# Slot attention stage of a decoder kernel on one Trainium2 core: four groups in turn in place of two, three units at once in a beat

## What is computed

```python
Pn = rmsnorm(P, input_norm_w); k_proj = Pn @ Wk.T; v_proj = Pn @ Wv.T
for _ in range(3):
    q_proj = rmsnorm(slots, slot_norm_w) @ Wq.T
    scores = einsum("bkd,bmd->bkm", q_proj, k_proj) * SCALE
    attn = softmax(scores, axis=-2)
    attn = attn / (sum(attn, axis=-1, keepdims=True) + EPS)
    updates = einsum("bkm,bmd->bkd", attn, v_proj)
    slots = gru_cell(updates, slots, ...)   # r, z: sigmoid; n = tanh(xn + r * hn)
x = layernorm(x + slots)
route = sigmoid(x @ Wr + br)                # the expert with the highest route takes the token
```

## Time and profile before

| | us |
|---|---|
| median of 3 runs | 1671.12 |
| the profiled execution, its own time | 1671.58 |
| its span, first to last instruction | 1669.4 |
| `slot_stage` | 918 to 1479 |
| TensorE busy over the span (89%) | 1489.2 |
| VectorE busy (76%) | 1262.5 |
| ScalarE busy (66%) | 1105.3 |
| POOL busy (75%) | 1246.7 |

### The profile page before, as it was taken

How to read it: one execution, slowest core, us unless ns; L and a number is a source line. 1 busy time by engine, 2 the same in 40 slices (tenths; PEclk the granted TensorE clock), 3 DMA queues, 4 the chain that set the end, 5 groups by cost and what they waited for, 6 DMA issues and landing times. The chain is left out here.

```text
span 1669.4 us, 22143 instructions
## 1 busy us (share of the span) xinstructions
PE 1489.2 (89%) x6336; PEld 908.0 (54%) x6336; DVE 1262.5 (76%) x2184; ACT 1105.3 (66%) x2134; POOL 1246.7 (75%) x884
## 2 busy tenths in 40 slices
PE   4889899989999999989987999999999999929994
PEld 1334334433443343433432777777777777729993
DVE  2999999999999999999996466666666675644552
ACT  4778887788778887888775665556556565414553
POOL 2899999999999999999996435666566655534665
PEclk8999999999999999999999899999999999959997
DMA  5455555554555455555551840412403310036771
GB/s 175 136 192 183 164 175 176 180 173 158 198 165 187 156 180 193 182 163 176 169 174 44 269 167 17 154 44 111 154 25 130 103 48 14 7 87 189 214 208 39
DMA packets 126058, 236.93 MB, mean 142 GB/s; under 512 B 13490, under 2 KB 76917, under 8 KB 125952
## 3 DMA queue, kind: packets, MB, share of 16 engines
q1 hardware_dynamic: 121408, 227.21, 41.8%
q0 software_dynamic: 4544, 8.47, 1.5%
HBM read 180.89 MB, written 55.66 MB: 142 GB/s over the span
## 5 line engine op out<-in xcount | busy, mean ns | idle before, releaser
L388 POOL TENSOR_TENSOR hc<-state,c_rows 128x1024 f32<-128x1024 f32 x256 | 599.1, 2362 | 50.0 <-DVE state L585 40.3
L585 DVE TENSOR_TENSOR_SCAN state<-ps_da,inp 128x512 f32<-128x512 f32 x512 | 593.5, 1207 | 29.6 <-ACT ps_da L481 29.6
L704 PE MATMUL ps_y<-hc,ident 128*128 128x512 f32 x1024 | 495.1, 623 | 55.5 <-POOL hc L388 55.4
L481 ACT ACTIVATE ps_da<-dt,a_neg 128x512 f32<-128x512 f32 x512 | 345.1, 688 | 81.7 <-DVE state L585 79.2
L704 PEld LDWEIGHTS ps_y<-hc,ident 128*128 128x128 f32 x1024 | 195.6, 198 | 298.8 <-issue 214.7
L574 DVE TENSOR_TENSOR inp<-dtx,ps_b 128x1024 f32<-128x1024 f32 x192 | 230.9, 1203 | 39.3 <-POOL dtx L359 23.0
L998 POOL TENSOR_TENSOR rs<-ms,m_half 128x4 f32<-128x4 f32 x48 | 49.7, 1035 | 186.4 <-DVE ms L1201 186.4
L371 POOL TENSOR_TENSOR inp<-dtx,b_rows 128x1024 f32<-128x1024 f32 x64 | 150.9, 2358 | 0.1
L627 PE MATMUL ps_misc<-x1T,w_conv 128*128 128x512 f32 (+3 forms) x256 | 118.6, 608 | 20.9 <-ACT x1T L414 20.9
L487 ACT COPY ps_b<-b_rows 128x512 f32<-128x512 f32 x192 | 111.1, 579 | 36.6 <-DVE inp L574 35.1
L1662 POOL DMA_INDIRECT out_x<-orow,target x78 | 77.0, 987 | 43.4 <-ACT orow L1681 23.7
(11 more groups left out here) (214 smaller groups left out, 2759.9 us busy)
## 6 DMA issues: line engine op xcount, KB each, us to landing
b_rows<-bc_rows SPq DMA_DIRECT2D x128, 512.0 KB, 4.7
c_rows<-bc_rows SPq DMA_DIRECT2D x128, 512.0 KB, 4.0
sorted_x<-pad_rows SPq DMA_DIRECT2D x8, 4160.0 KB, 16.3
w<-in_L_ffn_W SPq DMA_DIRECT2D x78, 256.0 KB
vw<-vw_rows SPq DMA_DIRECT2D x16, 462.0 KB
vw_rows<-vw_out SPq DMA_DIRECT2D x16, 384.0 KB
xrow<-sorted_x SPq DMA_DIRECT2D x39, 130.0 KB, 2.3
x_tok<-in_x SPq DMA_DIRECT2D x16, 256.0 KB, 4.0
```

The costliest lines, as they stand in the source:

```text
L388: pool.tensor_tensor(hc[:, n % RING], state[:, n % RING], over_c(c_rows[:, slot, n % 2]), ALU.mult).then_inc(hc_ready, 1)
L481: act.activation(ps_da[u % DA_RING][:], dt[:, par, c], ACT.Exp, scale=a_neg[:, c, n:n + 1]).then_inc(da_ready, 1)
L585: dve.tensor_tensor_scan(state[:, n % RING, c], ps_da[u % DA_RING][:], inp[:, n % RING, c], 0.0, ALU.mult, ALU.add).then_inc(state_ready, 1)
L704: ins = pe.matmul(ps_y[:, c], ident[:], hc[:, n % RING, c], start=False, stop=n == NS - 1)
```

## The change

The units of four groups follow each other: iteration 0 of groups 0 to 3, iteration 1 of groups 0 to 3, iteration 2, and then the next four. Each beat n holds the attention half of unit n up to the exponentials, the second part of the attention of unit n-1 (`den` to `weights`), and the GRU half of unit n-2, whose last steps (`gate_new`, `kept`, `mixed`, `new_h`) fall in beat n+1 of the loop as unit n-3. An iteration of a group therefore spans four beats. There are 48 beats with units and nine more in the loop. A group is routed in single steps, from `residual` at its ready beat (offset 0) to `scatter` (offset 6). For the first three fours, groups become ready three beats apart; the last four become ready in beats 47 to 50.

PSUM banks belong to a step and not to a lane: `ps_s` for scores, `ps_rs` for the spread root, `ps_d` for sums of squares, denominators and their spread, one `ps_u` that also takes the counts. `make_u` becomes two halves through the same columns. The two keep-running matmuls and `load_h` are gone: the first iteration reads `x1T` in place. `h`, `kq`, `vw` and `ctx_r` have eight buffers. The waits have semaphores by step. The core of the diff:

```diff
+    FOUR = 4
+    units = [(q * FOUR + k, j) for q in range(NG // FOUR) for j in range(ITERS) for k in range(FOUR)]
+    place_of = {unit: n for n, unit in enumerate(units)}
+    N = len(units)
+    ROUND = FOUR * ITERS
+    ready = {}
+    for g in range(NG):
+        spread = 2 * (g % FOUR) if g < NG - FOUR else 0
+        ready[place_of[g, ITERS - 1] + 3 + spread] = g
+    LAST = N + 9
...
-    ps_s = [psum(f"ps_s{k}", [P, T]) for k in range(2)]
+    ps_s = psum("ps_s", [P, T])
+    ps_rs = psum("ps_rs", [P, T])
+    ps_d = psum("ps_d", [P, T])
...
-    ps_u = [psum(f"ps_u{k}", [P, T]) for k in range(2)]
+    ps_u = psum("ps_u", [P, T])
+    COUNT_AT = 2 * (P + NE)
...
+    def h_in(n):
+        g, j = units[n]
+        return x1T[:, g * T:(g + 1) * T] if j == 0 else h[g % RING][:]
...
+    def root_at(g):
+        return g - 1 if g < FOUR else (g // FOUR - 1) * ROUND + ITERS * (g % FOUR) + 1
+    def ctx_parts(n):
+        for g in range(2, NG):
+            if n == max(0, root_at(g) - 2):
+                yield g, range(0, 2)
+            if n == max(0, root_at(g) - 1):
+                yield g, range(2, GB)
+    def ctx_roots(n):
+        for g in range(2, NG):
+            if n == root_at(g):
+                yield g
...
+        load_kq(1)
+        load_ctx(1)
+        load_vw(0)
+        for g in range(2, FOUR):
+            load_kq(g)
+            load_vw(g - 1)
+        load_ctx(2)
+        load_ctx(3)
+        load_vw(FOUR - 1)
...
+        for g in range(FOUR, RING):
+            load_ctx(g)
+            load_kq(g)
+            load_vw(g)
...
+        for n in range(LAST):
+            if live(n):
+                root(n)
+            if n == 0:
+                root_ctx(0)
+                root_ctx(1)
+            if live(n - 2):
+                halve(n - 2)
+            g = post(n, 0)
+            if g is not None and g < NG - 1:
+                residual(g)
+            g = post(n, 6)
+            if g is not None and g < NG - 2:
+                scatter(g)
+            g = post(n, 4)
+            if g is not None and g < NG - 2:
+                normed(g)
+            g = post(n, 2)
+            if g is not None:
+                logits(g)
+            g = post(n, 5)
+            if g is not None:
+                labels(g) if g < NG - 2 else last_labels(g)
+            for g in ctx_roots(n):
+                root_ctx(g)
...
+        for n in range(LAST):
+            if live(n - 3):
+                gate_new(n - 3)
+            if live(n):
+                copy_scores(n)
+            if live(n - 2):
+                gate_hn(n - 2)
+                gate_r(n - 2)
+            g = post(n, 1)
+            if g is not None:
+                read_u(g, 0)
+            if live(n + 1):
+                square(n + 1)
+            if live(n):
+                exps(n)
+            if live(n - 2):
+                gate_z(n - 2)
+            if g is not None:
+                read_u(g, 1)
+            g = post(n, 3)
+            if g is not None:
+                route_tanh(g)
+            for g, batches in ctx_parts(n):
+                sum_ctx(g, batches)
...
+        def last_norm(g):
...
+            dve.wait_ge(scattered[k], 16 * GB * (NQ - 1))
...
+        for n in range(LAST):
+            if live(n):
+                mean_sq(n)
+            g = post(n, 2)
+            if g is not None:
+                statistics(g)
+            if live(n - 3):
+                kept(n - 3)
+                mixed(n - 3)
+                new_h(n - 3)
+                if units[n - 3] == (NG - 1, ITERS - 1):
+                    last_residual(NG - 1)
+            if live(n):
+                maxima(n)
+            if live(n - 1):
+                denominators(n - 1)
+            if live(n - 2):
+                reset(n - 2)
+            if live(n - 1):
+                weights(n - 1)
+            g = post(n, 4)
+            if g is not None:
+                highest(g)
+                chosen_expert(g)
+                if g >= NG - 2:
+                    last_norm(g)
+            g = post(n, 5)
+            if g is not None:
+                ranks(g)
+                destinations(g)
+            if live(n):
+                normaliser(n)
+            if live(n - 2):
+                new_in(n - 2)
...
+        def count(g):
+            k, n = g % 2, NE * GB
+            need(pe, u_read, made_u[0])
+            need(pe, ranks_made, ev(RANKS, "base", made_counts[0] - 1))
+            pe.wait_ge(choice_made, ev(CHOICE, "upto", g))
...
-        def keep_running(lane, par, other, oit):
-            if other is not None:
-                pe.wait_ge(act2[other], ev(A2, "tz", oit))
-            pe.matmul(ps_z[:, 0:T // 2], whhT[:, P:2 * P], h[par][lane][:, 0:T // 2], start=True, stop=False, skip_group_check=True)
-        def keep_running_hn(lane, it, par):
-            pe.wait_ge(act2[lane], ev(A2, "hnb", it))
-            pe.matmul(ps_hn[:, T // 2:], whhT[:, 2 * P:], h[par][lane][:, T // 2:], start=True, stop=True)
...
+        for n in range(LAST):
+            if live(n - 2):
+                gate_hn(n - 2)
+                gate_h(n - 2, 0, ps_r, r_read)
+                gate_x(n - 2, 0, ps_r, r_full, True)
+            if live(n):
+                root_spread(n)
+            if live(n - 1):
+                den(n - 1)
+            if live(n - 2):
+                gate_h(n - 2, 1, ps_z, z_read)
+            g = post(n, 1)
+            if g is not None:
+                if g == 0:
+                    pe.wait_ge(prep_v, 5)
+                make_u(g, 0)
+            if live(n - 1):
+                den_spread(n - 1)
+            if live(n - 2):
+                gate_x(n - 2, 1, ps_z, z_full, True)
+                need(pe, pre_done, n - 2)
+                gate_x(n - 2, 2, ps_xn, xn_full, False)
+            if g is not None:
+                make_u(g, 1)
+            g = post(n, 4)
+            if g is not None:
+                count(g)
+            if live(n + 1):
+                ssq(n + 1)
+                scores(n + 1)
```

More of the change, by code:

```diff
@@ L786, in slot_stage @@
     at = [sb(f"at{k}", [M, T]) for k in range(2)]
+    half = [sb(f"half{k}", [P, T]) for k in range(2)]
     hnb = sb("hnb", [P, T])
@@ L826, in slot_stage @@
     ps_xn = psum("ps_xn", [P, T])
-    ps_u = [psum(f"ps_u{k}", [P, T]) for k in range(2)]
[L830 to L840, removed]
+    ps_u = psum("ps_u", [P, T])
+    COUNT_AT = 2 * (P + NE)
+    MOMENTS = ["stats", "mv"]
+    CHOICE = ["top", "less", "cand", "which", "hot", "upto"]
+    RANKS = ["based", "base", "chosen", "dest_f"]
+    LOGITS = ["veps", "rstd", "scaled", "logits"]
+    LABELS = ["gate", "id", "next_id"]
+    MAXIMA = ["s", "mx", "nmx"]
+    INVERSE = ["rse", "rser"]
+    STATE = ["keep", "mix", "h"]
+    w_in_place = sem("slot_w_loaded")
     const2 = sem("const2")
@@ new lines, in gate_new, with read_u, route_tanh @@
+        def gate_new(n):
+            act.wait_ge(pre_done, n + 1)
+            act.activation(nn[:], pre[:], ACT.Tanh, bias=bih[:, 2:3]).then_inc(new_read, 1)
+        def read_u(g, part):
+            act.wait_ge(u_full, 2 * g + part + 1)
+            need(act, rows_done, g - 1)
+            act.copy(tok[g % 2][:, 2 * part:2 * part + 2].rearrange("p b d -> p (b d)"), ps_u[:, 0:2 * (P + NE)]).then_inc(u_read, 1)
+        def route_tanh(g):
+            act.wait_ge(logits_made, ev(LOGITS, "logits", g))
+            need(act, choice_made, ev(CHOICE, "less", g - 2))
+            act.activation(route[g % 2][:], lg[g % 2][:], ACT.Tanh, scale=0.5).then_inc(routed, 1)
@@ L1412, in scores, with make_u @@
-        def scores(lane, it, j, q, par):
-            need(pe, dve1[lane], ev(V, "attn", it - 1))
-            if j == 0:
-                pe.wait_ge(kq_loaded[par][lane], 16 * (q // 2) + 16)
+        made_u = [0]
+        made_counts = [0]
+        def make_u(g, part):
+            k = g % 2
+            need(pe, u_read, made_u[0])
+            need(pe, ranks_made, ev(RANKS, "base", made_counts[0] - 1))
+            if g < NG - 1:
+                pe.wait_ge(summed, g + 1)
+            else:
+                pe.wait_ge(last_summed, 1)
+            for b in range(2 * part, 2 * part + 2):
+                at_col = (b % 2) * (P + NE)
+                ins = pe.matmul(ps_u[:, at_col:at_col + P + NE], res2[k][:, b * P:(b + 1) * P], w_rows[:], start=True, stop=True)
+            ins.then_inc(u_full, 1)
+            made_u[0] += 1
@@ L1507, in _ @@
-        over_pairs(pe, body)
-        it = NQ * ITERS - 1
-        pe.wait_ge(post_v[1], ev(POSTV, "base", NQ - 2))
-        gate_x(1, it, 1, "r")
-        gate_x(1, it, 1, "z")
-        gate_x(1, it, 1, "xn")
-        for lane in range(2):
-            make_u(NQ, lane)
-        count(0, NQ - 1, 1, it)
-        pe.wait_ge(post_v[0], ev(POSTV, "base", NQ - 1))
-        count(1, NQ - 1, 1, it)
+        pe.wait_ge(w_in_place, 16 * 4)
+        pe.matmul(ps_u[:, 0:NE], ones[:], w_r[:], start=True, stop=True).then_inc(prep_pe, 1)
```

801 lines of the change are left out of this document (324 added, 477 removed).

## The result

| | kernel before | changed kernel |
|---|---|---|
| median of 4 runs, us | 1672.29 (1670.48 to 1673.56) | 1694.16 (1692.41 to 1699.39) |
| ratio to before, 95% interval | | 1.0137 (1.0112 to 1.0162) |
| profiled execution, us | 1671.58 | 1693.93 |
| its span, us | 1669.4 | 1691.7 |
| mean granted clock of TensorE | 0.953 | 0.922 |

What follows compares the result with a forecast made beforehand. It took TensorE as the bound, working 9.77 of a 10.14 us beat. Beats -55.3, start +17.8, tail +37.2 and clock +6 gave +5.7 on 1671.1, so 1676.8 us; 8-in-10 range 1656 to 1702.

Steps and rivals of the forecast that it cites:

- 1, the steady beat: Plain beats without routing work: 9.25 us, 0.9 less than now, including a new wait of 0.36 at den_spread.
- 2, the routing beat: Every third beat from 15 on: 12.0 us, count waiting 1.5 for ScalarE's second copy; with plain beats, gain 55.3.
- 3, the start: First beats: context 4 lands behind page 0, product 1 at 954.4, product 3 at 974.0 against 956.20; loss 17.8 us.
- the rival that it lands beside the page: Start: context 4 lands beside page 0, product 3 comes 15 us earlier, total 1661.8; chance 0.15.
- 4, the tail: After the last beat's product: 66.1 us through GpSimd's queue, last norms and scatters, against 28.85 now; loss 37.2 us.
- 5, the clock: TensorE's granted clock in the 11 routing beats: two falls of 3.0 us each; loss 6 us.
- The rival with a fall in every routing beat: Clock falls in every routing beat and some plain ones: 11 x 3.4 in place of 6, total 1708; chance 0.15.
- the beat stays as long as now: Steady part: a wait counted as slack is late, 0.4 more in 45 beats, +18, total 1695; chance 0.10.

Runs made afterwards that it cites:

- run without fillers: Kernel before without the keep_running and keep_running_hn matmuls, whose results nobody reads: 1688.82 us, ratio 1.0132 to the kernel before.
- both edits of the start: Changed kernel with spare-row and page-0 writes behind loads of groups 4 to 7, 1679.13 us; or context 4 summed in beats 3 and 4, 1676.98 us.
- Four buffers: Changed kernel with four buffers, not two, for tok and for its means and inverse deviations: 1682.69 us.
- run 1694: The changed kernel itself, with no follow-up edit, against the kernel before: median 1694.16 us, ratio 1.0137.

## Why the prediction was right in sign and short in size

It said 1676.8 (slower, chance 0.55, range 1656 to 1702); the median was 1694.16. By its steps, forecast and measured:

- **1, the steady beat**: 9.25, measured 9.18 to 9.34, and the new wait at `den_spread` is there, 0.24 on average (7.7 us in 32 waits) and 0.4 at most, where the sum had 0.36. Right. But one sentence before it was wrong: that TensorE was the bound of the kernel before. The run without fillers shows that its beat of 10.14 stayed when 0.88 of work left, and that the waits for `rse`, the roots and the squares grew in its place. That the chain through them set the beat follows from these waits. The subtraction gave the right number because in the new order TensorE is the bound.
- **2, the routing beat**: 12.0, measured 11.68 where the clock holds; beat 12 9.8, measured 9.78. The count waits for ScalarE's second copy as said, 1.06 and not 1.5. Beats together -58.5 against -55.3.
- **3, the start**: loss 17.8, measured 19.6; product 1 forecast 954.4, came at 953.31, behind the load named. Shown by both edits of the start. Context 4 was issued 5.3 us behind page 0 and came in at 951.53, 15.5 after its issue and 1.0 behind the page (950.5); with the writes behind it, it took 2.8. So the rival that it lands beside the page falls. The Trainium skill (DMA: Bandwidth & Descriptors, Queues, rings and completion order) has descriptors consumed in ring order on each DMA engine; the trace agrees. The sum left out that the load also waits for the sums of context 2, which cost nothing here, since the page ahead of it landed only at 950.5.
- **4, the tail**: loss 37.2, measured 43.9 (72.1 and not 66.1 to the end of the last destination, and 1.05 more to the next stage). The chain of the two last norms and scatters is there (6.07 and 5.65 of waiting), but the cast of scatter 12 came 50.8 behind product 47, not 42.8. Residual 14 still ended at 18.2, as forecast 18.0, so the 8 us lie in the queue behind it. I took GpSimd's queue as full and missed that `read_u` waits for the normalising of the group two before. ScalarE's copies stood 8.5 and 7.0, and GpSimd itself twice stood idle 3.85, waiting for what was late through its own queue. Four buffers took 7.8 out and brought the cast to 42.96. A norm took 3.14, not 4, and the two scatters that VectorE waited for landed 2.4 behind their last issue, not 3.7, which hid part of the miss. The other part not in the sum is that the stage ends by GpSimd, not by the last destination.
- **5, the clock**: loss 6, measured 16.8. **This is the term that was furthest off.** Two falls of 3.0 were taken, seven came, of 1.68 or 3.35. The place was named rightly, the idle time beside narrow matmuls in every routing beat; the earlier trace rows gave the size of a fall and not how often it comes. The rival with a fall in every routing beat gives a total that is nearer (1708 is 13.8 off, 1676.8 is 17.4), but its term of 37 is further from 16.8 than the 6 is; other terms' misses make up for it.

The misses, 10.8, 6.7, 1.8, 0.6 and -3.2, add up to the 16.7 between +5.7 and +22.4. That "the beat stays as long as now" gives 1695 and the run 1694 is chance: no beat was late by it.

Reading x1 in place was priced at nothing and not tried alone; the steady beat, met to 0.1 us, leaves little room for a cost there. Why seven of eleven beats fell and not all (five to eight in the other runs) stays open.

## What to carry to other kernels

When an engine's work per step is meant to be the bound, place each step's odd extra work (here the count) where its inputs have long been ready, behind work that is ready anyway: moving three small matmuls behind two groups of others was worth 32 us. A faster steady part buys nothing if the pipeline fills later and drains longer: read both ends apart, ask which load the first beats wait for and what stands ahead of it in its queue, and how many buffers back the last groups reach. Filling work is not dead weight until a run without it says so.

## What the runs showed that I had not expected

- A wait of 1.06 us on TensorE with narrow matmuls behind it was followed by up to 6.9 us at 1.2 GHz, in 7 of 11 cases. One matmul of 0.86 us put into it brought the clock back to 1.00, and 19.5 us. The Trainium skill (TensorE: Matmul & The Clock Gate, HAM oscillation — how this bites in real kernels) tells of falls behind waits for loads; here the wait was for a copy.
- The next stage began 4.92 us behind GpSimd's last instruction in every kernel of the new order (1495.50 to 1500.42, 1483.74 to 1488.65, 1429.09 to 1434.00), in the first of these although VectorE worked until 1499.37. In the kernel before GpSimd was done at 1473.23, and the stage began 5.46 behind it and 0.40 behind VectorE's last (1478.29). So an engine that ends early enough hides these 4.9 us. I have no row that says what GpSimd does in it.
- VectorE normalised a group in 1.1 us where GpSimd took 3.13.
